# Query norms moved from a multiply on POOL into the scale and bias of the exponentials

## The reference, cut to what matters

```
q = l2norm(q) * qs            # t / clip(norm(t), 1e-12), per token and head
k = l2norm(k) * ksc
q, k = rotary_xpos(q, k)      # q * cos * scale + rotate_half(q) * sin * scale
sim = einsum(q * 8, k)        # 64 queries against 128 keys
attn = softmax(where(mask, -max, sim))
out = attn @ v
```

## Time and profile before

| | us |
|---|---|
| median of 3 runs | 424.98 |
| lowest, highest | 422.65, 426.35 |
| the profiled execution | 424.36 |
| its span, first to last instruction | 422.2 |
| busy: PE | 364.5 (86%) |
| busy: DVE | 293.7 (70%) |
| busy: ACT | 297.3 (70%) |
| busy: POOL | 257.5 (61%) |

### The profile page before, as it was taken

How to read it: one execution, slowest core, us unless ns; L and a number is a source line. 1 busy time by engine, 2 the same in 40 slices (tenths; PEclk the granted TensorE clock), 3 DMA queues, 4 the chain that set the end, 5 groups by cost and what they waited for, 6 DMA issues and landing times. The chain is left out here.

```text
span 422.2 us, 10798 instructions
## 1 busy us (share of the span) xinstructions
PE 364.5 (86%) x3999; PEld 277.9 (66%) x3999; DVE 293.7 (70%) x525; ACT 297.3 (70%) x909; POOL 257.5 (61%) x232
## 2 busy tenths in 40 slices
PE   1737855799999999998969878799999999988995
PEld 0626644578888888876636446688888888765563
DVE  4797875587787777864745766678777787565363
ACT  2334651689999898998617468889989899974621
POOL 2173589598888888892003548988888888710000
PEclk9976995899999999999989989999999999999999
DMA  8920000123232232231320003123223222110001
GB/s 294 347 77 2 2 2 2 37 53 74 50 73 61 57 71 53 63 71 33 92 121 0 0 0 77 44 55 71 57 57 73 51 68 66 46 36 12 25 25 50
DMA packets 34514, 25.80 MB, mean 61 GB/s; under 512 B 18933, under 2 KB 29087, under 8 KB 33951
## 3 DMA queue, kind: packets, MB, share of 16 engines
q1 hardware_dynamic: 34175, 24.66, 21.8%
q10 hardware_dynamic: 288, 0.46, 0.4%
HBM read 9.64 MB, written 1.05 MB: 25 GB/s over the span
## 5 line engine op out<-in xcount | busy, mean ns | idle before, releaser
L1006 ACT ACTIVATE probs<-ps,neg_max 128x128 f32<-128x128 f32 x256 | 90.1, 378 | 5.5 <-DVE neg_max L1229 4.4
L531 POOL TENSOR_TENSOR qkn<-rot 128x512 f32<-128x512 f32 x64 | 80.5, 1280 | 11.7 <-PE ps L728 4.1
L539 POOL TENSOR_TENSOR qkn<-qkn,rnorm 128x512 f32<-128x512 f32 x64 | 65.5, 1045 | 22.9 <-ACT rnorm L956 22.9
L545 POOL TENSOR_TENSOR probs_n<-probs,row_inv 128x512 f32<-128x512 f32 x64 | 66.6, 1042 | 19.1 <-DVE row_inv L1234 16.2
L1006 ACT ACTIVATION_READ_ACCUMULATOR probs<-ps,neg_max 128x1 f32 x256 | 55.4, 216 | 0.0
L949 ACT ACTIVATE sq<-ps 128x1024 f32<-128x1024 f32 x32 | 32.8, 1026 | 30.0 <-DVE rot L1181 19.2
L520 POOL TENSOR_TENSOR h_lo<-xin,h_hi 64x512 fp32r<-64x512 f32 x16 | 20.6, 1290 | 43.1 <-DVE sin_w L1189 26.9
L1229 DVE TENSOR_REDUCE neg_max<-ps 128x4 f32<-128x512 f32 x64 | 41.0, 681 | 8.3 <-PE ps L742 8.3
L173 PE MATMUL ps<-wqkv_hi,h_hi 128*128 128x512 f32 x96 | 42.8, 446 | 0.0
L1181 DVE TENSOR_TENSOR rot<-ps,cos_w 128x1024 f32<-128x1024 f32 x32 | 39.1, 1221 | 3.6 <-PE ps L175 3.0
L1171 DVE TENSOR_REDUCE ss<-sq 128x16 f32<-128x1024 f32 x32 | 38.8, 1212 | 3.9 <-ACT sq L949 3.8
(11 more groups left out here) (127 smaller groups left out, 806.1 us busy)
## 6 DMA issues: line engine op xcount, KB each, us to landing
v_off<-v_tok SPq DMA_DIRECT2D x64, 128.0 KB, 2.3
k_t<-k_t SPq DMA_DIRECT2D x30, 128.0 KB, 2.3
cos_w<-in_cos_t SPq DMA_DIRECT2D x2, 1024.0 KB, 7.9
sin_w<-in_sin_t SPq DMA_DIRECT2D x2, 1024.0 KB, 9.5
x_shift<-x SPq DMA_DIRECT2D x64, 32.0 KB, 1.9
x_raw<-in_x SPq DMA_DIRECT2D x4, 256.0 KB, 4.7
out<-o_t SPq DMA_DIRECT2D x4, 256.0 KB, 2.3
x_shift<-in_wqkv SPq DMA_DIRECT2D x1, 768.0 KB, 7.4
```

The costliest lines, as they stand in the source:

```text
L531: pool.tensor_tensor(to, first, second[:, :, ::-1, :], ALU.add).then_inc(rot_summed, 1)
L539: pool.tensor_tensor(of, of, rnorm[:, part * HEADS:(part + 1) * HEADS].unsqueeze(2) .broadcast_to([P, HEADS, DH]), ALU.mult).then_inc(rot_ ...
L545: pool.tensor_tensor(probs_n[:, 4 * g:4 * g + 4, :], probs[:, 4 * g:4 * g + 4, :], row_inv[:, 4 * g:4 * g + 4].unsqueeze(2).broadcast_to([ ...
L1006: e = act.activation(probs[:, k, :], s_ps[g][:, cw * P:(cw + 1) * P], ACT.Exp, bias=neg_max[:, k:k + 1], accum_out=row_sum[:, k:k + 1])
```

## The change

POOL's multiply covers the keys alone (`scale_keys`). The queries stay unscaled: PE turns them as soon as POOL has summed them. The inverse norms of the queries enter in two places. Each exponential gets rnorm of its head as per-partition scale, beside the per-partition bias. The bias has to be the negated maximum times the same rnorm: DVE computes it after each of the two maxima in a new instruction (`scale_maxima`, 128x4, L1240 of the changed kernel), which waits for the maximum, and the exponentials wait for it. rnorm is now needed until the exponentials of its tile, so there are two buffers, and ACT's Exp of the norms waits for the keys of two tiles before. The counts of the semaphore rot_scaled follow.

```diff
-        rnorm = sb("rnorm", [P, 2 * HEADS])
+        rnorm = [sb(f"rnorm{i}", [P, 2 * HEADS]) for i in range(2)]
...
+        exp_bias = sb("exp_bias", [P, 8])
...
-            def scale_rotated(n):
+            def scale_keys(n):
 
                 after(pool, rnorm_done, n + 1)
-                for part in range(2):
-                    after(pool, rot_summed, 2 * n + (part + 1))
-                    of = qkn[:, part * INNER:(part + 1) * INNER].rearrange("p (h d) -> p h d", d=DH)
-                    pool.tensor_tensor(of, of, rnorm[:, part * HEADS:(part + 1) * HEADS].unsqueeze(2)
-                                       .broadcast_to([P, HEADS, DH]), ALU.mult).then_inc(rot_scaled, 1)
+                after(pool, rot_summed, 2 * n + 2)
+                of = qkn[:, INNER:].rearrange("p (h d) -> p h d", d=DH)
+                pool.tensor_tensor(of, of, rnorm[n % 2][:, HEADS:].unsqueeze(2)
+                                   .broadcast_to([P, HEADS, DH]), ALU.mult).then_inc(rot_scaled, 1)
...
-                    after(pe, rot_scaled, 2 * n + (part + 1))
+                    if part == 0:
+                        after(pe, rot_summed, 2 * n + 1)
+                    else:
+                        after(pe, rot_scaled, n + 1)
...
-                after(act, rot_scaled, 2 * n)
-                act.activation(rnorm[:], lnss[:], ACT.Exp, scale=-0.5, bias=eps_s[:, 1:2]).then_inc(rnorm_done, 1)
+                after(act, rot_scaled, n - 1)
+                act.activation(rnorm[n % 2][:], lnss[:], ACT.Exp, scale=-0.5, bias=eps_s[:, 1:2]).then_inc(rnorm_done, 1)
...
-                    after(act, max_done, 2 * n + (g + 1))
+                    after(act, bias_done, 2 * n + (g + 1))
                     after(act, probs_n_done, 2 * n + (g - 1))
                     for cw in range(4):
-                        k = 4 * g + cw
+                        k, head = 4 * g + cw, 2 * cw + g
                         e = act.activation(probs[:, k, :], s_ps[g][:, cw * P:(cw + 1) * P], ACT.Exp,
-                                           bias=neg_max[:, k:k + 1], accum_out=row_sum[:, k:k + 1])
+                                           bias=exp_bias[:, k:k + 1], scale=rnorm[n % 2][:, head:head + 1], accum_out=row_sum[:, k:k + 1])
...
+                def scale_maxima(n, g):
+                    after(dve, rnorm_done, n + 1)
+                    after(dve, max_done, 2 * n + (g + 1))
+                    after(dve, probs_done, 2 * n + (g - 1))
+                    dve.tensor_tensor(exp_bias[:, 4 * g:4 * g + 4], neg_max[:, 4 * g:4 * g + 4],
+                                      rnorm[n % 2][:, g:HEADS:2], ALU.mult).then_inc(bias_done, 1)
...
                         maxima(n, 0)
-                    if there(t):
+                        scale_maxima(n, 0)
                         maxima(n, 1)
+                        scale_maxima(n, 1)
```

More of the change, by code:

```diff
@@ L382, in build @@
         max_done = sem("max_done")
+        bias_done = sem("bias_done")
         probs_done = sem("probs_done")
@@ L555, in step @@
                         sum_rotated(n + 1)
-                        scale_rotated(n + 1)
+                        scale_keys(n + 1)
                     if there(t):
@@ L560, in step @@
                     if layer > 0 and t == 0:
-                        pool.wait_ge(rot_scaled, 2 * n + 4)
+                        pool.wait_ge(rot_scaled, n + 2)
                         pool.wait_ge(probs_n_done, 2 * n + 2)
@@ L571, in _ @@
                     sum_rotated(n0)
-                    scale_rotated(n0)
-                    pool.wait_ge(rot_scaled, 2 * n0 + 2)
+                    scale_keys(n0)
+                    pool.wait_ge(rot_scaled, n0 + 1)
                     split_input(layer, SPANS - 2)
@@ L593, in _ @@
                 if layer < LAYERS - 1:
-                    pool.wait_ge(rot_scaled, 2 * (n0 + TILES))
+                    pool.wait_ge(rot_scaled, n0 + TILES)
         @block.tensor
```

## The result

The changed kernel takes 478.75 us (median of four runs, 475.55 to 480.85) against 425.67 us (four runs, 422.65 to 426.44): 1.1255 times the time before, 95% interval 1.1158 to 1.1352. The forecast was 452.9, from 446 to 463. The direction is right; the amount isn't: it grew by 53 us and not by 28. The profiled execution took 480.85 us, which is 56.5 more than the profiled one of before.

The account below looks back on a forecast made before the run. PE bound most of the loop at 7.63 us per tile, the ACT-DVE ring close behind at 7.49, becoming 8.51. Terms 12.9 + 11.6 + 2.0 + 0.4 + 1.6 = 28.5 on 424.36 gave 452.9 us, range 446 to 463.

Parts of the forecast that it names:

- a wait on DVE's own result some 0.03: Between the maximum's end and DVE's new product: a delay of some 0.03 us, within the product's 0.21.
- the second rival: POOL's key multiply starts before DVE's product, which waits for all of it: +1.0 for 28 intervals, 481 us; chance 0.08.
- the CAST: DVE instruction at 232.84 in the earlier trace, taking its usual 0.42 beside POOL's h_lo; cited for DVE going first.
- The second pointer: On ACT's exponentials, the added per-partition scale costs 0.10 us each, eight per tile: +0.80 in the ring.
- The product: DVE's 128x4 multiply between maximum and exponentials: 0.21 us itself, path from ssc 1.09 instead of 0.87, +0.22.
- The ring: ACT and DVE's loop from one tile's exponentials to the next: 7.49 + 0.80 + 0.22 = 8.51 us, above PE's 7.63.
- The hold: DVE's product kept waiting by POOL's work: forecast none, as DVE is 0.05 us ahead, except in layer 1's second tile.
- Layer 1's second tile, +0.7: There POOL's order puts half the rotation sum, 1.28 us, over the product: +0.7 us once.
- The sixteenth tiles: Last tile of each layer, without rotation: 0.80 + 0.22 at most per layer, +2.0 for both.
- The end: Behind each layer's last exponentials, PE's wait for probs_n: the 0.80 passes through, +1.6 for both layers.
- POOL's relief at nothing: Removing 32 POOL multiplies of 1.045 us gains nothing, as they lie beside PE's work and the ring.
- The third rival: PE's granted clock falls because PE now has gaps; one tile in ten at half speed is +21, some 475 us; chance 0.04.

Follow-up runs that it names:

- the two experiments: Changed kernel with DVE's two long-met waits moved ahead of the maximum: 452.59 us; changed kernel with POOL's key multiply waiting for the product: 453.05 us.
- the settled waits first: Against the changed kernel, DVE's waits for the norms and for earlier exponentials moved ahead of the maximum; 452.59 us, 1.064 times the kernel before.
- the experiment with neither part: Changed kernel without product and per-partition scale, POOL multiplying the keys alone, queries' norm scaling left out; 424.04 us, 0.999 times the kernel before.
- the keys in two halves: Changed kernel with POOL's key multiply split into two instructions of 256 columns; 468.02 us.
- both maxima first: Changed kernel with both products placed behind both maxima in DVE's order; 485.04 us.

## Why the prediction was wrong

The step that failed is the smallest number in it: "a wait on DVE's own result some 0.03". From it came a product issued 0.86 to 0.87 after ssc, 0.05 ahead of POOL's 0.91, and from that the forecast that DVE wins. It measures 0.08, since three waits stand ahead of the product where the row behind which 0.03 is seen has one. The product is issued at 0.91 and POOL at 0.90. POOL was in its place to 0.01 us; DVE wasn't. The rest follows as the second rival put it, who gave 481 us and a chance of 0.08. That chance was far too small. That its time is so near the measured one is in part luck: it had 28 tiles of 1.0 us, and there are 25 of 0.88, 6 us less; the profiled execution makes that up with 7 us of lower clock, named below. A margin of 0.05 that rests on an estimate of 0.03 is as good as none, and the CAST in the earlier trace rows showed only who wins with DVE ahead, not that DVE would be ahead. The diff named the three waits.

By its steps:

- The second pointer, 0.80 per tile (0.10 each): 0.085 each in the instruction's duration, 0.72 per tile in the ring. Right in kind, a tenth too large. The Trainium skill, ScalarE: Activation LUTs, section "What ACT_TABLE_LOAD costs", has about 93 ns for each pointer operand, by which eight are an estimated 0.74; the trace is near it, with 0.085 in the duration and 0.09 of the ring for each. (The prediction put the sum by that figure at 451.7; its own terms give 451.1.)
- The product, +0.22 with 0.21 for itself: 0.20 where nothing holds it, and 0.25 with its three waits. Right.
- The ring without the hold, 8.51: 8.42 and 8.48 in the two experiments. Their 452.59 and 453.05 us are near the 452.9 of the forecast, nearer than its terms bear out, which is luck: the profiled executions took 450.84 and 454.73 us, the ring is 0.09 and 0.03 shorter, and in the second of them the way to layer 1 takes 63.8 us where the forecast has 60.9. (The prediction's bounds of the ring, 8.38 and 8.74, add up to 8.36 and 8.72 from its own terms; the range hardly moves.)
- The hold, forecast as zero in all tiles but one: 25 tiles of 0.88, 22 us. The rest of the miss goes with PE's granted clock: the 3.7 of the front, the 0.9 of layer 0's second tile, and the 2.5 by which the way to layer 1 was longer than its term. Over all ten profiles that way follows the clock granted on it and not the edits: 59.9 to 60.9 us at 0.94, 61.4 and 62.3 at 0.92, 63.2 to 63.8 at 0.89, 65.3 at 0.87. Take the 22 and these three from the 56.5, and 27.4 are left, where the sum said 28.5.
- Layer 1's second tile, +0.7 by POOL's sum over the rotations. Right. The product there takes 0.67, under the first of POOL's two sums, and its interval is 9.12, as it is with the settled waits first, where the others are 8.42:

```profile
296.51 0.67 DVE L1240 TENSOR_TENSOR exp_bias<-neg_max,rnorm 128x4 f32<-128x4 f32 x1
```

- The sixteenth tiles, 1.0 each: 9.20 against 8.24. Right.
- The end, 0.8: the second reciprocal comes 3.66 after the first exponential (2.93 in the earlier trace rows), and PE's wait for probs_n grows from 0.74 to 1.10. The last exponentials and what follows, in time:

```profile
427.18 0.46 ACT L1010 ACTIVATE probs<-ps,exp_bias,rnorm 128x128 f32<-128x128 f32 x1 [1.11 <-DVE exp_bias L1240]
...
430.84 0.18 DVE L1245 RECIPROCAL row_inv<-row_sum 128x4 f32<-128x4 f32 x1 [1.58 <-ACT probs L1010]
...
432.19 0.66 PE L760 MATMUL ps<-small,probs_n 128*128 128x128 f32 x4 [1.10 <-POOL probs_n L546]
```

- POOL's relief at nothing: the experiment with neither part says the same, 0.999.
- The third rival, the clock: in the loops it stayed at 0.99 and 1.00 with PE busy for 83% of them, and fell in one tile alone. It didn't decide, but it isn't nothing: with the front and the way to layer 1 the lower clock goes with 7 of the 56.5 us, and the forecast had no term for it.

The Trainium skill, SBUF — State Buffer, section "Who interferes with whom", says that a Vector instruction with two SBUF inputs and a GpSimd one that reads SBUF exclude each other, and that the order of issue decides. The trace agrees on DVE's side: behind by 0.01 the product takes 1.04 us, ahead by 0.04 to 0.08 it takes 0.16. On POOL's side no wait shows here: with the product 0.04 ahead and 0.12 us of overlap, POOL's multiply takes the 1.04 that it takes without a product. The rule was cited in the prediction, and then its question was answered with the wrong 0.05.

## What to carry to other kernels

When two engines exclude each other and their starts are as near as the 0.05 us here, price both orders as about equally likely, unless a row shows the start behind just as many waits. A tiny DVE instruction with two SBUF inputs on the path costs its own 0.16 us or all that is left of what POOL has under way, here up to 1.04: give it an order against POOL by a wait, or issue its settled waits early. And before work is taken off an engine, look whether that engine is late anywhere; here POOL was in one tile alone (0.8 us), while the exponentials that took the work over pay 0.72 us in each tile.

## What was not expected of the hardware

Waits that have been met aren't free: two of them ahead of the product moved its start from 0.03 to 0.08 us after the instruction that it waits for (the second experiment against the changed kernel; the two weren't moved one by one).

DVE's product 0.04 ahead of POOL isn't held and doesn't slow POOL (1.04 in both orders), unlike the CAST in the earlier trace rows, which was ahead by 0.01 and beside which POOL's instruction took 1545 ns and not 1274; 0.01 behind, the product waits for the whole instruction. It also gets in between two POOL instructions that follow each other at once (0.62).

TensorE's granted clock fell in single places of some kernels. With the keys in two halves it is 0.68 in the stretch from 208.7 to 214.0, shown there, so part of it ran at 1.2 GHz and not at 2.4. Before it PE had been idle for 1.92 us (the wait of its instruction at 208.77). The changed kernel has the same place at 219.9:

```profile
219.88:225.18 5.30, 4.90 (x53) 3.36 (x54) 2.06 (x4) 4.16 (x11) 0.57 (x1) 1.00 0.23 51
```

It had been idle for 2.37 us there, and the clock stays at 1.00. With both maxima first PE is idle for 2.36 us at the same place (until 216.19), and the clock falls:

```profile
216.20:221.50 5.30, 5.08 (x45) 3.00 (x47) 0.83 (x2) 3.47 (x7) 0.21 (x1) 0.68 0.23 53
```

So the gap alone doesn't decide. The lower clock goes with the longer sixteenth tiles of those two experiments (10.9 and 11.3 us against 9.2). What tips it stays open.
